# A four-block graph network on one core: the set-up stretch ahead of the loop is issued in another order

## The reference

```
x = layernorm(x + adj @ (x @ W) + bias)                          # L0, all 512 nodes
x = layernorm(x + fused(x))                                      # L1, changes nodes 0 to 24 only
    # 5 groups g of nodes, idx_g: A = adj[idx,idx] + I, normed by degree on both sides
    # h = relu(A' @ (x[idx] @ W1[g]) + b1[g]);  out = relu(A' @ (h @ W2[g]) + b2[g])
    # fused[idx] += softmax(fusion_w)[g] * out
x = layernorm(x + attention(x))                                  # L2: a = adj * exp(e_i + f_j), rows normed
x = layernorm(x + gru(conv branch, message branch, x))           # L3: convolutions of 1 and 17 taps, a GRU cell
```

## Time and profile before

| | us |
|---|---|
| median of 3 runs | 574.63 (573.37 to 574.97) |
| the profiled execution | 573.76 |
| its span, first to last instruction | 572.0 |
| outside the span | 1.76 |
| end of TensorE's set-up work | 68.67 |
| first matmul of the loop | 69.92 |
| TensorE busy in the span | 552.4 (97%) |
| VectorE busy | 479.0 (84%) |
| ScalarE busy | 398.9 (70%) |
| GpSimd busy | 218.7 (38%) |

### The profile page before, as it was taken

The page is one execution under the profiler, slowest core; times in us unless marked ns, Lnnn a source line. Parts: engine busy times, 40 slices in busy tenths (PEclk is TensorE's granted clock), DMA queues, the critical chain, the costliest instruction groups (busy, mean ns, idle before and its releaser), DMA issues.

```text
span 572.0 us, 12140 instructions
## 1 busy us (share of the span) xinstructions
PE 552.4 (97%) x3639; PEld 488.0 (85%) x3639; DVE 479.0 (84%) x1764; ACT 398.9 (70%) x844; POOL 218.7 (38%) x213
## 2 busy tenths in 40 slices
PE   7879999999999999999999999999999999999994
PEld 6767898988989898989888898989898988989684
DVE  3897778889898988889888989898888888898665
ACT  2467576767877868777677778687777777786452
POOL 3312025253533434352535344443525353443010
...
DMA packets 33302, 34.46 MB, mean 60 GB/s; under 512 B 1664, under 2 KB 22532, under 8 KB 33147
## 3 DMA queue, kind: packets, MB, share of 16 engines
...
...
...
## 4 chain that ended last, share of the span: by engine, by line
PE 85%; DVE 1%; ACT 1%; issue 0%; POOLq 0%; POOL 0%; DVEq 0%
PE bank L264 14%; PE bank L266 14%; PE bank L265 14%; PE pair L264 6%; PE pair L266 6%; PE pair L265 6%; PE bank L1673 5%; PE bank L1684 3%; PE bank L1777 2%; PE pair L1833 2%; PE pair L1765 2%; PE bank L1868 2%; PE bank L1869 2%; PE bank L1872 2%; PE bank L1738 1%; PE bank L1848 1%
## 5 line engine op out<-in xcount | busy, mean ns | idle before, releaser
L1161 POOL TENSOR_TENSOR rs<-ve,neg_half 128x4 f32<-128x4 f32 (+1 forms) x60 | 55.2, 921 | 135.4 <-DVE ve L1397 101.1
L1195 POOL TENSOR_TENSOR P_lo<-P,P_hi 128x512 fp32r<-128x512 f32 x56 | 82.0, 1484 | 49.7 <-ACT P_hi L1234 49.7
L264 PE MATMUL bank<-cd_hi,w_hi 128*128 128x256 f32 x272 | 77.2, 284 | 0.0
L265 PE MATMUL bank<-cd_lo,w_hi 128*128 128x256 f32 x272 | 76.5, 281 | 0.0
L266 PE MATMUL bank<-cd_hi,w_lo 128*128 128x256 f32 x272 | 76.2, 280 | 0.0
L1432 DVE TENSOR_TENSOR P<-bank,aT 128x512 f32<-128x512 f32 x64 | 41.2, 685 | 17.5 <-ACT bank L1220 17.4
L264 PE MATMUL pair<-aT_hi,x_hi 128*128 128x512 f32 x128 | 52.5, 410 | 1.4 <-DVE x_lo L810 1.4
L265 PEld LDWEIGHTS bank<-cd_lo,w_hi 128*128 128x128 f32 x272 | 51.2, 188 | 1.6
L264 PEld LDWEIGHTS bank<-cd_hi,w_hi 128*128 128x128 f32 x272 | 51.3, 189 | 1.5
L266 PEld LDWEIGHTS bank<-cd_hi,w_lo 128*128 128x128 f32 x272 | 51.5, 189 | 0.0
L266 PE MATMUL pair<-aT_hi,x_lo 128*128 128x512 f32 x128 | 50.5, 394 | 0.0
...
## 6 DMA issues: line engine op xcount, KB each, us to landing
...
```

What stands on the lines that cost most here:

```text
L264: nc.tensor.matmul(o, lh, rh, start=start, stop=False)
L265: nc.tensor.matmul(o, lh, rl, start=False, stop=False)
L1161: g.tensor_tensor(rs[i][:, 0:n], ve[i][:, 0:n], neg_half[:, 0:n], ALU.pow).then_inc(po_rs[i], 1)
L1195: g.tensor_tensor(P_lo[:, mc, :], P[:, mc, :], f(P_hi[:, mc, :]), ALU.subtract).then_inc(po_Plo[mc], 1)
```

## The change

Six edits, all in the set-up:

1. The 14 loads of `vrows` leave SP's queue and are issued on ACT's, behind `x_hi`. The two tiny broadcasts (`fw`, `ab_col`) go behind `nat_ws`, and SP's wait for `adjP` goes. So `hw1` and all that follows stands directly behind `xt[0]`.
2. VectorE prepares `nat_w1`, `nat_wm`, `nat_ws` right behind `hT0` and ahead of the wait for GpSimd's root of the degrees.
3. The last two products of graph 0's layer 1 are released in two pieces (groups 0 and 1; groups 2 to 4), with their banks divided anew.
4. The two reductions over the groups become additions: three for `hsum`; for the last step a pair, `tmp0[4]` into `fused_in`, one, and the final sum.
5. VectorE makes `x_lo` ahead of the own rows' sum, statistics and norm; one `scale_columns` goes behind the dot product, `nat_c1` behind `x_lo`.
6. TensorE transposes the first eight weight blocks behind graph 0's second product, and ScalarE rounds them behind the 17 taps and the copy of that product.

```diff
+        sum2 = R2[:, 0:2, :]
...
-        NAT_BANK, TT_BANK = bank[4], bank[5]
+        NAT_BANK, TT_BANK = bank[4], bank[6]
...
                 x_tile(0)
-                for row, name, n in ((A1, "L2_gnn_a_w", 2), (WB, "L2_gnn_W_b", 1), (G1, "L3_gnn_bn1_g", 1),
...
-                    sp.dma_start(vrows[row:row + n, :], a[name].rearrange("(n d) -> n d", n=n)).then_inc(q_row, 16)
-                sp.dma_start(vrows[BMSG:NROWS, :], a["L3_gnn_b_msg"].unsqueeze(0)).then_inc(q_row, 16)
-                sp.dma_start(vrows[HB:BMSG, :], a["L1_gnn_b1"].rearrange("g (h d) -> (g h) d", h=2)).then_inc(q_row, 16)
-                for dst, src in ((fw[:, 0, :], a["L1_gnn_fusion_w"].partition_broadcast(128)),
-                                 (ab_col[:, :], a["L2_gnn_a_b"].partition_broadcast(128))):
-                    sp.dma_start(dst, src).then_inc(q_cst2, 16)
-                sp.wait_ge(q_adjP, 32 * PJ)
                 sp.dma_start(hw1[:, :, :], a["L1_gnn_W1"].rearrange("g i h -> i g h")).then_inc(q_h1, 16)
...
                 sp.dma_start(nat_ws[0:3, 0:1], a["L3_gnn_b_se"].unsqueeze(1)).then_inc(q_ww, 16)
+                for dst, src in ((fw[:, 0, :], a["L1_gnn_fusion_w"].partition_broadcast(128)),
+                                 (ab_col[:, :], a["L2_gnn_a_b"].partition_broadcast(128))):
+                    sp.dma_start(dst, src).then_inc(q_cst2, 16)
                 sp.dma_start(hb2[:, :, :], a["L1_gnn_b2"].partition_broadcast(128)).then_inc(q_cst2, 16)
...
                 act.wait_ge(x_in[0], 16)
                 s.activation(x_hi[:, :, :], x_nat[0][:, :, :], ACT.Identity).then_inc(ac_xhi, 1)
+                for row, name, n in ((A1, "L2_gnn_a_w", 2), (WB, "L2_gnn_W_b", 1), (G1, "L3_gnn_bn1_g", 1),
...
+                    act.dma_start(vrows[row:row + n, :], a[name].rearrange("(n d) -> n d", n=n)).then_inc(q_row, 16)
+                act.dma_start(vrows[BMSG:NROWS, :], a["L3_gnn_b_msg"].unsqueeze(0)).then_inc(q_row, 16)
+                act.dma_start(vrows[HB:BMSG, :], a["L1_gnn_b1"].rearrange("g (h d) -> (g h) d", h=2)).then_inc(q_row, 16)
...
                 act.wait_ge(q_S0, 1)
-                s.activation(S0[0:NODES, 0:4, :], bank[5][0:NODES, :].rearrange("p (g d) -> p g d", g=4), ACT.Identity)
-                s.activation(S0[0:NODES, 4, :], bank[6][0:NODES, 0:D], ACT.Identity).then_inc(q_S0s, 1)
+                s.activation(S0[0:NODES, 0:2, :], bank[5][0:NODES, 0:2 * D].rearrange("p (g d) -> p g d", g=2),
+                             ACT.Identity).then_inc(q_S0s, 1)
+                act.wait_ge(q_S0, 2)
+                s.activation(S0[0:NODES, 2:NG, :], bank[6][0:NODES, 0:3 * D].rearrange("p (g d) -> p g d", g=3),
+                             ACT.Identity).then_inc(q_S0s, 1)
                 scale_rows(2)
                 scale_rows(3)
                 copy_natural()
...
                     s.activation(aT[1][:, mc, :], AT_BANK[mc % 2][:, :], ACT.Identity).then_inc(ac_aT[mc], 1)
-                round_weights(0)
-                round_weights(1)
                 scale_taps()
                 act.wait_ge(pe_agg2, 1)
                 s.activation(agg_sb[:, :], AG_BANK[:, :], ACT.Identity).then_inc(ac_agg2, 1)
+                round_weights(0)
+                round_weights(1)
                 for t in range(PT):
                     copy_u(t)
                 act.wait_ge(dv_e, 1)
...
                 v.tensor_scalar(hT0[:, :, :], hT0[:, :, :], 0.0, None, ALU.max).then_inc(q_own, 2)
+                dve.wait_ge(q_ww, 16 * 4)
+                dve.nop(nofuse=True)
+                v.tensor_scalar(nat_w1[:, 1:D], nat_ww[:, 0, 1:D], nat_ww[:, 0, 0:1], None, ALU.subtract)
...
+                v.tensor_scalar(nat_ws[0:3, 1:D], nat_se[0:3, 1:D], nat_se[0:3, 0:1], None, ALU.subtract).then_inc(q_sc1, 1)
                 inverse_degrees(R, NG, NT * NG, 2)
...
-                v.reduce_sum(hsum[0:R, :], hb2[0:R, :, :].rearrange("p g d -> p d g"), X).then_inc(q_fuse, 1)
+                v.tensor_tensor(sum2[0:R, :, :], hb2[0:R, 0:2, :], hb2[0:R, 2:4, :], ALU.add).then_inc(q_fuse, 1)
                 dve.wait_ge(q_fuse, 7)
+                v.tensor_tensor(hsum[0:R, :], sum2[0:R, 0, :], sum2[0:R, 1, :], ALU.add).then_inc(q_fuse, 1)
+                dve.wait_ge(q_fuse, 8)
+                v.tensor_tensor(hsum[0:R, :], hsum[0:R, :], hb2[0:R, 4, :], ALU.add).then_inc(q_fuse, 1)
+                dve.wait_ge(q_fuse, 9)
                 dve.wait_ge(dv_x1, 1)
                 v.tensor_tensor(fused_in[0][:, :], x1[0:NODES, 0, :], hsum[0:NODES, :], ALU.subtract).then_inc(q_x1c, 1)
...
                     last = dot(1, c)
                 last.then_inc(q_own, 1)
-                dve.wait_ge(q_ww, 16 * 4)
...
-                v.tensor_scalar(nat_ws[0:3, 1:D], nat_se[0:3, 1:D], nat_se[0:3, 0:1], None, ALU.subtract).then_inc(q_sc1, 1)
                 dve.wait_ge(q_own, 4)
-                dve.wait_ge(q_o0, 1)
-                dve.nop(nofuse=True)
                 for gi in range(NG):
-                    o = bank[7][0:NODES, ch(gi)] if gi < 4 else bank[6][0:NODES, 0:D]
+                    hold(dve, q_o0, 1 if gi < 2 else 2)
+                    o = bank[7][0:NODES, ch(gi)] if gi < 2 else bank[5][0:NODES, ch(gi - 2)]
                     last = v.scalar_tensor_tensor(tmp0[0:NODES, gi, :], o, wm[0:NODES, gi:gi + 1], hb2[0:NODES, gi, :],
                                                   ALU.mult, ALU.max)
                 last.then_inc(q_own, 1)
                 dve.wait_ge(q_own, 5)
-                v.reduce_sum(red0[0:NODES, :], tmp0[0:NODES, :, :].rearrange("p g d -> p d g"), X).then_inc(q_own, 1)
+                v.tensor_tensor(sum2[0:NODES, :, :], tmp0[0:NODES, 0:2, :], tmp0[0:NODES, 2:4, :], ALU.add).then_inc(q_own, 1)
+                dve.wait_ge(q_x1c, 1)
+                v.tensor_tensor(fused_in[0][:, :], fused_in[0][:, :], tmp0[0:NODES, 4, :], ALU.add).then_inc(q_x1c, 1)
                 dve.wait_ge(q_own, 6)
-                dve.wait_ge(q_x1c, 1)
+                v.tensor_tensor(red0[0:NODES, :], sum2[0:NODES, 0, :], sum2[0:NODES, 1, :], ALU.add).then_inc(q_own, 1)
+                dve.wait_ge(q_own, 7)
+                dve.wait_ge(q_x1c, 2)
                 dve.wait_ge(q_U0, 1)
                 v.tensor_tensor(x1[0:NODES, 0, :], red0[0:NODES, :], fused_in[0][:, :], ALU.add).then_inc(dv_fused, 1)
...
                 v.tensor_scalar(ve[1][:, 0:1], mv[1][:, 0, 1:2], EPS, None, ALU.add).then_inc(dv_ve[1], 1)
                 scale_columns(1)
-                scale_columns(2)
...
                 v.tensor_scalar(gate_bias[:, 2:3], cols[:, BHH + 2:BHH + 3], 0.5, None, ALU.mult).then_inc(q_gb, 1)
-                dve.wait_ge(q_wt, 16 * 3)
-                dve.nop(nofuse=True)
-                v.tensor_scalar(nat_c1[:, :], nat_c1[:, :], bn_scale[:, 0:1], None, ALU.mult).then_inc(q_sc1, 1)
                 hold(dve, po_rs[1], 1)
                 v.tensor_scalar(x2[:, 0, :], x1[:, 0, :], mv[1][:, 0, 0:1], rs[1][:, 0:1], ALU.subtract,
                                 ALU.mult).then_inc(dv_x2, 1)
                 hold(dve, dv_x2, 1)
                 dot(1, 0).then_inc(dv_f, 1)
+                scale_columns(2)
+                hold(dve, ac_pf, 1)
+                v.tensor_copy(x_hi[:, :, 0], pef[:, 1, :]).then_inc(dv_pfh, 1)
+                dve.wait_ge(dv_pfh, 1)
+                v.tensor_tensor(x_lo[:, :, 0], pef[:, 1, :], f(x_hi[:, :, 0]), ALU.subtract).then_inc(dv_pf, 1)
+                for c in range(NC):
+                    hold(dve, ac_xs[c], 1)
+                    v.scalar_tensor_tensor(x_lo[:, c, 1:D], x2[:, c, 1:D], pef[:, 1, c:c + 1], f(x_hi[:, c, 1:D]),
+                                           ALU.mult, ALU.subtract).then_inc(dv_xs[c], 1)
+                dve.wait_ge(q_wt, 16 * 3)
+                dve.nop(nofuse=True)
+                v.tensor_scalar(nat_c1[:, :], nat_c1[:, :], bn_scale[:, 0:1], None, ALU.mult).then_inc(q_sc1, 1)
                 dve.wait_ge(q_o, 1)
                 dve.wait_ge(q_xPb, 1)
                 v.tensor_tensor(x1P[0:R, :, :], bank[7][0:R, 0:PT * D].rearrange("p (t d) -> p t d", t=PT), xP[0:R, :, :],
...
                 last.then_inc(q_nP, 1)
-                hold(dve, ac_pf, 1)
-                v.tensor_copy(x_hi[:, :, 0], pef[:, 1, :]).then_inc(dv_pfh, 1)
...
-                    v.scalar_tensor_tensor(x_lo[:, c, 1:D], x2[:, c, 1:D], pef[:, 1, c:c + 1], f(x_hi[:, c, 1:D]),
-                                           ALU.mult, ALU.subtract).then_inc(dv_xs[c], 1)
                 hold(dve, q_nP, 2)
...
                 for gi in range(NG):
-                    o = bank[5][0:NODES, ch(gi)] if gi < 4 else bank[6][0:NODES, 0:D]
+                    o = bank[5][0:NODES, ch(gi)] if gi < 2 else bank[6][0:NODES, ch(gi - 2)]
                     for h in range(2):
                         last = t_.matmul(o, hT0[:, 2 * gi + h, :], hw2[:, gi, h, :], start=(h == 0), stop=(h == 1))
-                last.then_inc(q_S0, 1)
+                    if gi in (1, NG - 1):
```

(18 more changed lines are left out.)

18 lines of the change are left out of this document (6 added, 12 removed).

## The result

The changed kernel takes 572.56 us (median of 20 runs, 571.62 to 574.90), the kernel before on the same chip 574.00 (20 runs, 573.00 to 575.49). The ratio is 0.9973, with a 95% interval from 0.9963 to 0.9982. So the change is worth about 1.5 us, between 1.0 and 2.1. The loop is as before: its first matmul starts at 68.06 instead of 69.92, and the profiled execution takes 571.94 us, 1.82 less than before.

The account below looks back on a forecast made before the run. VectorE's work between 28.77 and 45.76, up to the own rows' norm, was taken to bound the set-up; its terms gave -0.93 us, the collision +0.55, so -0.38: 574.2 us from 574.63, range 572.0 to 575.6.

Parts of the forecast that it names:

- the second product's chain: Rival in the set-up: graph 0's second product decides, up to 2.5 us gained, 572.1 us; chance 0.12.
- TensorE's last wait ahead of the barrier: TensorE ahead of `x1P`: stands still about 1.2 us instead of 0.54, waiting for VectorE's norm.
- The `nat` block: VectorE's `nat` preparation, moved ahead of its wait for GpSimd's root and hidden there: -0.70 us.
- `hsum`: On VectorE, one reduction of 1.26 us becomes three additions, 1.07 with pauses: -0.22 us.
- the last step of layer 1: Graph 0 on VectorE: reduction and sum of 1.62 us become additions of about 1.15: -0.47 us.
- The exposed wait ahead of `tmp0`: On VectorE, nothing covers the three dot products ahead of the `tmp0` step any more: +0.11 us.
- ScalarE's pace: Early `x_lo` on VectorE must keep pace with ScalarE's four `x_hi`, 1.27 us: +0.16 us.
- the statistics: On VectorE, the aggregation now waits for the statistics, 0.68 us and a pause of 0.11: +0.19 us.
- the collision: GpSimd's `xP` addition, moved to about 34.0, blocks VectorE's new pair addition with both operands in SBUF: +0.55 us.
- the slow rival: Every GpSimd operation, the root too, blocks VectorE's SBUF operations: +0.67 us, 575.3 us; chance 0.08.
- for `xt` this removes TensorE's 1.44 us: Later loads land 3.1 us earlier; TensorE's wait for `xt` at 35.05 goes but was hidden, so worth 0.
- pauses of 1.44 and 1.42 us: TensorE's idling for `xt` and `x_lo` left the clock at 1.00, so longer idling ahead of `x1P` costs 0.

Follow-up runs that it names:

- the old order: The changed kernel with edits 5 and 6 undone (`x_lo` behind the own rows' statistics again): 572.88 us, ratio 0.9963 to the kernel before.
- GpSimd's root first: GpSimd's root for graph 0's second norm ahead of its `xP` addition: in the changed kernel 573.71 us, 0.9981; with edits 5 and 6 undone 571.66 us, 0.9963.
- the provoked ones: Collisions in the changed kernel with one more GpSimd addition (125x384, SBUF operands) released beside VectorE's sums on purpose: 573.28 us, one run.
- the swapped kernel: The changed kernel with edit 1 undone and GpSimd's root for the second norm ahead of its `xP` addition: 574.56 us, ratio 1.0001.
- the first experiments: Follow-ups with 35 runs of the kernel before beside them (median 573.95 us); among them edit 1 alone on the kernel before, 573.45 us, ratio 0.9978.

## Why the prediction was right, and where it was wrong

The verdict that it gave (no difference that a measurement can tell, somewhat faster) held, and the time lies in the range. The working behind it was mostly right on VectorE and wrong on what decides. That 572.56 lies in the range is luck in part: the range reaches down to 572.0 only for the rival in which the second product's chain decides, and that is not what happened. TensorE's last wait ahead of the barrier is for VectorE's norm, 1.35 us at 43.97, as forecast (1.2).

**Right: VectorE's sum, nearly term by term.** The `nat` block gave 0.70 (forecast 0.70), `hsum` 0.18 (0.22), the last step of layer 1 0.49 (0.47), the split in two pieces nothing. The exposed wait ahead of `tmp0` costs 0.21 (0.11), ScalarE's pace 0.24 (0.16). All of it together is -0.72 where -0.93 was forecast without a collision; that these are so near is luck, as two errors of 0.37 and 0.38 us cancel (next paragraph).

**Wrong in size: the statistics.** Forecast were 0.19 us for uncovering them, from a pause of 0.11 between dependent operations. Measured: 0.56, as the aggregation starts 0.47 us behind the end of three statistics. The pause of 0.11 was read behind one statistic. What the old order hid was thus more than I counted. At the same time the 0.38 us ahead of the norm, for which the trace of before names nobody, are gone. They go in the old order too, when only the sums are changed, so they are not tied to edit 5; what they are stays open. By the rows the new order loses by itself: 9.85 us from L771 to the norm, against 9.04 in the old one (its 9.85 less the 0.81 of the collision). The times point the same way in both pairs (0.9963 against 0.9973, and 0.9963 against 0.9981 with GpSimd's root first), but their intervals overlap.

**Wrong in chance, right in mechanism: the collision.** I put +0.55 us on it. In the profiled execution of the changed kernel it costs nothing, by 0.12 us. With the old order it costs 0.81, near the top of my range for it (0.9), and the provoked ones cost 0.81 and 0.69. So the mechanism is shown. Its price is what is left of GpSimd's addition when VectorE's operation comes: 0.7 to 0.8 us where they start together, 0.44 where VectorE's came in the middle (the transfers put back), nothing where `xP` lands too early or too late. The Trainium skill (SBUF — State Buffer, section "Who interferes with whom") has it so: the engine that issues first holds the shared pair of ports for its whole instruction, and the other is blocked. The trace agrees where VectorE meets GpSimd's addition, down to two columns (0.93 us for an addition of 128x2, 0.98 for a scalar operation). It disagrees where the GpSimd operation is the root of the degrees: the `nat` rows take 0.28 us inside it (24.79 to 27.55), as `hT` did before. Of the two `hT` is the firmer case: for a scalar operation the rule asks for a two-port mode, and it is `hT`, with 250 columns in 0.29 us, that runs faster per column than the 127 of `nat` in 0.28. Of the slow rival, which needed both, half was therefore true.

**Wrong, and this is the step that failed: "for `xt` this removes TensorE's 1.44 us, which was hidden anyway", the transfers at 0.** The runs show the reverse. The transfers alone give 0.9978; VectorE's first three edits alone give 1.0001; all but the transfers give 1.0000. (Each of the last two intervals still has room for some 0.9 us of gain; with the swapped kernel's 1.0001 it is three that centre on none. What VectorE's edits add on top of the transfers can't be told either: 0.9973 against 0.9978.) I had read the 1.44 us in one execution, and in that one the set-up ahead had been held up by the stretch of low clock from 11 to 15 us, so that `xt` was late by little. When the set-up is on time, the wait grows to 1.88 us, two others appear (0.87 and 0.74 us), and TensorE, having idled, may get the lower clock behind them. My reading is that late transfers set a floor under the time, and that what VectorE saves stays under it. Among the executions whose mean granted clock was 0.997 or more, the changed kernel stood at 571.6 to 572.7 (11 of its 20 runs), and with the transfers put back three stood at 574.0 to 574.7, no faster than the rest. But it is not one floor for all: the kernel before, with the same late transfers, stood at 572.6 to 573.2 in five such executions of the same rounds. So at the full clock VectorE's edits with late transfers stood above the kernel before, by 1.4 us on average (three executions against five), and by which operation stays open. Of the ways in which they can cost time the rows show three, each in single executions: TensorE's wait for `xt` with a lower clock behind it, `xP` beside VectorE's operations, and the root behind `xP`.

**Not thought of: that the clock in the set-up is uneven between executions.** I wrote that pauses of 1.44 and 1.42 us left the granted clock at 1.00 and cost it at 0. This was true of the trace, though the same trace has it at 0.59 from 11 to 15 us, behind a pause of 1.89. In two of the kernels above it fell behind a pause of 1.88 and of 1.32 us, and stayed up behind 1.83 and 2.27. Of the 1.84 us between the two profiles, 1.12 lie ahead of the root's end, where one of them has such a stretch, and 0.72 are VectorE's. Of the 20 runs of the changed kernel 11 had a mean granted clock of 0.997 or more, of the 35 of the kernel before beside the first experiments, in other rounds, 3. That such stretches are rarer with the transfers ahead is not shown: with edit 1 alone it was 1 of 12, with the old order and the transfers ahead 2 of 12, with the transfers put back 2 of 12 and 1 of 12. How much of the gain comes through the clock stays open. The profiles' difference of 1.8 us is close to the measured gain of 1.5, but it is one execution against one.
